# Two mask buffers, and the mask's DMAs issued by ScalarE

## The chip, the cores and the metric

The kernel runs on one core of a Trainium2 chip. The metric is the device time of one execution in microseconds (us). The engines are PE (TensorE: matmuls into PSUM), DVE (VectorE), ACT (ScalarE), POOL (GpSimd) and SP (SyncE, which here only issues DMAs). Each runs its own list of instructions in order. They wait for each other by semaphores, which count up.

## The reference, cut to what matters

A deformable convolution on 8 images of 16 x 16 pixels and 64 channels is followed by an attention and a mixture of experts on the tokens. Only the convolution matters here:

```
xdw    = depthwise_conv3x3(group_norm(x)) + dw_b
om     = xdw @ om_w + om_b            # per pixel, 8 groups, 9 taps: offset x, offset y, mask
value  = group_norm(x) @ vp_w + vp_b  # 8 groups of 8 channels
for each group g, tap k, pixel:
    sample value[g] bilinearly at (pixel + tap k + offset), zero outside the image
    out[g] += sample * mask[g, k]
x = x + out @ op_w
```

## The kernel before, in words

The bilinear weights are written as hats: the weight of image row y is max(0, 1 - |py - y|), and the same for columns. For an image, `a` holds the hats of rows for 128 partitions (8 groups x 16 rows), 9 taps and 256 pixels; `b` holds those of columns. `a` is also multiplied by the mask, so that the sum over rows and columns is the whole of the convolution.

For image n the steps are:

- PE multiplies `om_w` by the convolved image, in two halves (`offsets`, line 272). ACT copies them with a bias to `om_f` (`copy_offsets`, line 488) and rounds them to `om_r` (`high_offsets`, line 502); POOL makes the rest of the rounding (`low_offsets`).
- The mask is part of `om_f`. Three DMAs (`masks`, line 233) bring it to the 128 partitions of `mask`: three taps each, 384 KB, where each of 8 source rows goes to 16 partitions. SP issues them.
- PE spreads the offsets to the partitions in nine steps (`replicate`) through one bank, `ps_m`. ACT copies each out as |.| (`copy_rep`) and makes the hat (`hat`). Five of the nine fill `a`, in pairs of taps.
- POOL multiplies a pair of taps of `a` by `mask` (`masked`, line 762), when the hat is there and the mask's DMA has landed.
- SP copies each pair of `a` to `a_rep` by four DMAs (`fill`, line 241), each from 32 partitions to 128. There are two buffers, by the image's parity. 16 of the 20 DMAs have 256 KB, the last pair's four 128 KB.
- PE samples columns into PSUM (`sample`), DVE multiplies by `a_rep` (`weight`, 18 products an image, line 663), and PE sums over rows into `ps_d` (`reduce`).

The order is written out by hand. While PE, DVE and ACT are at image i, PE puts the spreading of image i + 1 between its batches (`JOBS`, line 195), and ACT and POOL make `a` and `b` of image i + 1. SP's list is: masks of image n, fills of image n, masks of n + 1, and so on. With one `mask`, the masks of image n + 1 may be written only when POOL has done the last multiplication of image n; SP's place behind the last `fill` of image n, which waits for `a_done`, sees to this. ACT writes `om_f` of image n only when the masks of image n - 1 have landed (`mask_in`, line 494) and when POOL has done all multiplications of image n - 1 (`a_done`, line 495).

Tile names: `ps_t`, `ps_m`, `ps_d` are in PSUM, `prod` holds products; `om_copied` counts halves of `om_f`, `a_done` pairs multiplied by the mask, `weighted` products.

Of the kernel before, what the change touches and what calls it, by code (L numbers as in the profile page):

```python
# [27 lines left out]
ALU = mybir.AluOpType  # L28
# [3 lines left out]
P = 128  # L32
IMAGES, H, W, C = 8, 16, 16, 64
PIX = H * W
TT = IMAGES * PIX // P
TPI = PIX // P
GROUPS = 8
GC = C // GROUPS
TAPS = 9
# [4 lines left out]
QUADS = 3  # L44
# [3 lines left out]
MASK_ROWS = [slice(0, 64, 8), slice(1, 64, 8), slice(64, 114, 7)]  # L48
PLACE_ROWS = {0: [r for r in range(64) if r % 8 > 1], 64: [r for r in range(64, 120) if r % 7 != 1 or r > 113]}
BANK = 512  # L50
PAIRS = (TAPS + 1) // 2
# [8 lines left out]
def positive(value):  # L60

    return not isinstance(value, int) or value > 0

def count(eng, value):

    return value if isinstance(value, int) else eng.snap(value)

def spread(ap, dim, n):  # L70

    ap = ap.unsqueeze(dim)
    return ap.broadcast_to([n if k == dim else size for k, size in enumerate(ap.shape)])
# [18 lines left out]
def conv_stage(nc, d, t_tok, pack, pack_in):  # L92

    with ExitStack() as ctx:
        def sb(name, shape, dt=F32, where=ctx):
            return where.enter_context(nc.sbuf_tensor(name, shape, dt))

        def sem(name):
            return ctx.enter_context(nc.semaphore(name))  # L100
# [35 lines left out]
        om_f = sb("om_f", [P, QUADS, PIX])  # L136
# [2 lines left out]
        vt = [sb(f"vt{i}", [P, 2, DUO, H, 4]) for i in range(2)]  # L139
        a = sb("a", [P, TAPS, PIX])  # L140
        b = [sb(f"b{i}", [P, TAPS, PIX]) for i in range(2)]
        mask = sb("mask", [P, TAPS, PIX])
        a_rep = [sb(f"a_rep{i}", [P, DUOS, TAPS, PIX]) for i in range(2)]
        prod = [sb(f"prod{i}", [P, 2, BANK]) for i in range(PROD)]
        d_sb = sb("d_sb", [P, BANK])
# [21 lines left out]
        om_copied = sem("om_copied")  # L167
# [10 lines left out]
        a_done = sem("a_done")  # L178
        b_done = sem("b_done")
        mask_in = [sem(f"mask_in{j}") for j in range(QUADS)]  # L180
# [34 lines left out]
        def pair_taps(k):  # L215

            return slice(2 * k, min(2 * k + 2, TAPS))
# [7 lines left out]
        @block.sync  # L225
        def _(sp):
            sp.dma_start(x_turned[:, :, :, :].rearrange("p s y x -> p (s y x)"), d["x_turned"]).then_inc(x_in, 16)
            sp.dma_start(keep[:, :], d["keep"]).then_inc(keep_in, 16)
            sp.dma_start(start[:, :], d["start"]).then_inc(start_in, 16)
            sp.dma_start(t_tok[:, :, :], xview).then_inc(tokens_in, 16)  # L230
            sp.dma_start(pack[:, :], d["attention"]).then_inc(pack_in, 16)

            def masks(n):

                sp.wait_ge(om_copied, 2 * n + 2)
                for j in range(QUADS):
                    src = om_f[MASK_ROWS[j], :, :].rearrange("g q x -> g (q x)")
                    sp.dma_start(mask[:, QUADS * j:QUADS * (j + 1), :].rearrange("p q x -> p (q x)"),
                                 src.unsqueeze(1).broadcast_to([GROUPS, P // GROUPS, QUADS * PIX])).then_inc(mask_in[j], 16)

            def fill(n, par):

                used = count(sp, WPI * (n - 1))
                if positive(used):
                    sp.wait_ge(weighted, used)
                for k in range(PAIRS):
                    sp.wait_ge(a_done, PAIRS * n + k + 1)
                    for m in range(DUOS):
                        src = a[32 * m:32 * m + 32, pair_taps(k), :]
                        sp.dma_start(a_rep[par][:, m, pair_taps(k), :],  # L250
                                     src.unsqueeze(1).broadcast_to([32, 4, src.shape[1], PIX]))\
                          .then_inc(a_filled[k][m // 2], 16)

            masks(0)
            fill(0, 0)
            masks(1)
            fill(1, 1)
            with sp.Fori(1, IMAGES // 2) as it:
                for par in range(2):
                    masks(2 * it + par)  # L260
                    fill(2 * it + par, par)

        @block.tensor
# [207 lines left out]
        def _(act):  # L471
# [16 lines left out]
            def copy_offsets(half, n):  # L488
                act.wait_ge(om_ps, 2 * n + half + 1)
                if positive(2 * n + half - 1):  # L490
                    act.wait_ge(om_low, 2 * n + half - 1)
                if positive(n) and half == 0:
                    for j in range(QUADS):
                        act.wait_ge(mask_in[j], 16 * n)
                    act.wait_ge(a_done, PAIRS * n)
                bank = ps_m[:, :] if positive(n) else ps_t[0][:, half, :]
                for q in range(2 - half):
                    op = act.activation(om_f[0:ROWS, 2 * half + q, :], bank[0:ROWS, q * PIX:(q + 1) * PIX],  # L498
                                        ACT.Identity, bias=om_bias[0:ROWS, 2 * half + q:2 * half + q + 1])
                op.then_inc(om_copied, 1)  # L500

            def high_offsets(half, n):
                act.wait_ge(om_copied, 2 * n + half + 1)
                if positive(len(REPS) * n):
                    act.wait_ge(rep_ps, len(REPS) * n)
                act.activation(om_r[0:ROWS, 2 * half:2 + half, :], om_f[0:ROWS, 2 * half:2 + half, :],
                               ACT.Copy).then_inc(om_high, 1)
# [67 lines left out]
            def image(i, par, slab, made):  # L575
                n, npar = i + 1, 1 - par
                if made:
                    copy_offsets(0, n)
                    high_offsets(0, n)
                last = None if isinstance(i, int) and i == 0 else i - 1  # L580
                if LAG == 1 and last is not None:
                    copy_d(last)
                if made:
                    copy_offsets(1, n)
                    high_offsets(1, n)
                if LAG == 2 and last is not None:
                    copy_d(last)
                if made:
                    reps(n, npar, slab)
# [9 lines left out]
            high_offsets(0, 0)  # L599
            copy_offsets(1, 0)  # L600
            high_offsets(1, 0)
            first_reps()
            image(0, 0, 1, True)
            image(1, 1, None, True)
# [127 lines left out]
        @block.gpsimd  # L732
        def _(pool):
            pool.memset(minus_half[:, :], -0.5).then_inc(zeroed, 1)
            pool.memset(xpad[:, :, :, :], 0.0).then_inc(zeroed, 1)
            pool.wait_ge(zeroed, 2)
            pool.wait_ge(gn_steps, 5)
            pool.tensor_tensor(grstd[:, :], gvar_eps[:, :], minus_half[:, :], ALU.pow).then_inc(gn_pow, 1)

            def low_offsets(half, n):  # L740

                if half == 0 and positive(n):
                    pool.wait_ge(a_done, PAIRS * n)
                pool.wait_ge(om_high, 2 * n + half + 1)
                q = slice(2 * half, 2 + half)
                pool.tensor_tensor(om_r[64:ROWS, q, :], om_f[64:ROWS, q, :], om_r[64:ROWS, q, :].bitcast(F32),
                                   ALU.subtract).then_inc(om_low, 1)

            def tables(n, par, slab):

                pool.wait_ge(keep_in, 16)
                pool.wait_ge(om_low, 2 * n + 2)
                pool.wait_ge(v_done, slab + 1)
                if positive(WPI * (n - 1)):
                    pool.wait_ge(sampled, WPI * (n - 1))
                for j in range(DUO):
                    op = pool.tensor_tensor(vt[par][:, :, j, :, :].rearrange("p h y c -> p y h c"),
                                            v_sb[:, :, par, j, :].rearrange("p y (h c) -> p y h c", h=2),
                                            spread(spread(spread(rows[:, j], 1, H), 2, 2), 3, 4), ALU.mult)
                op.then_inc(vt_ready, 1)  # L760

            def masked(k, n, par):

                pool.wait_ge(a_hat, PAIRS * n + k + 1)
                for j in range(2 * k // QUADS, min(2 * k + 1, TAPS - 1) // QUADS + 1):
                    pool.wait_ge(mask_in[j], 16 * (n + 1))
                v = a[:, pair_taps(k), :]
                pool.tensor_tensor(v, v, mask[:, pair_taps(k), :], ALU.mult).then_inc(a_done, 1)  # L768

            def image(n, par, slab):  # L770
                low_offsets(0, n)
                low_offsets(1, n)
                tables(n, par, slab)
                for k in range(PAIRS):
                    masked(k, n, par)

            image(0, 0, 0)
            image(1, 1, 0)
            image(2, 0, 1)
            with pool.Fori(1, IMAGES // 2 - 1) as it:  # L780
                image(2 * it + 1, 1, it)
                image(2 * it + 2, 0, it + 1)
            image(IMAGES - 1, 1, SLABS - 1)
# [849 lines left out]
```

## Time and profile before

| | us |
|---|---|
| median of 3 runs (476.04 to 477.93) | 477.06 |
| the profiled execution | 478.97 |
| its span in the trace | 477.1 |
| busy: PE / DVE / ACT / POOL | 406.5 / 331.4 / 237.9 / 136.3 |
| products of DVE, line 674: 128 of them | 152.6, 1.219 each |

The convolution takes the span's first 276 us, the tokens the rest. A busy share is an average over both. What an engine waited for, and when, is read from its rows in order of time, where a bracket tells the idle time ahead of a row and what ended it.

### The profile page before, as it was taken

The page shows a single profiled execution, that of the slowest core. Times are in us where ns is not written, and L with a number is a line of the kernel's source. Part 1 is how long each engine was busy: PE and PEld are TensorE (multiplying, and loading weights), DVE is VectorE, ACT ScalarE, POOL GpSimd, SP SyncE. Part 2 cuts the span into 40 slices and gives each one's busy share as a digit, 9 for nine tenths or more (in the row PEclk, how much of TensorE's full clock was granted, in tenths as well). Part 3 has the DMA queues.
Part 4 walks back from the last instruction along what each step waited for, and adds up shares of the span by engine and source line. Part 5 has one row for each costly group of instructions (what it writes and reads, how often), then busy time and mean ns, then how long its engine had stood idle before and what let it go on. Part 6 is the DMA issues. An engine that isn't in the chain of part 4 may idle for free. (4 is left out here: it accounts for less than half of the span.)

```text
span 477.1 us, 9502 instructions
## 1 busy us (share of the span) xinstructions
PE 406.5 (85%) x3188; PEld 222.6 (47%) x3188; DVE 331.4 (69%) x725; ACT 237.9 (50%) x528; POOL 136.3 (29%) x172
## 2 busy tenths in 40 slices
PE   0739989799999899998969745899999999999995
PEld 0612343332433324332323234776676767777673
DVE  3417978569886498876957845668696967768653
ACT  3543544335544256353530034567767676776752
POOL 2242160421503315133040044223332323223322
PEclk9967999979999599998987955589999999999998
DMA  7178687796976968869789060000000000000000
GB/s 215 31 181 222 154 217 209 159 247 143 231 210 154 237 155 218 217 140 229 170 201 239 14 264 1 0 3 0 2 3 11 2 0 3 12 0 3 12 0 13
DMA packets 31672, 53.94 MB, mean 113 GB/s; under 512 B 7056, under 2 KB 11280, under 8 KB 31376
## 3 DMA queue, kind: packets, MB, share of 16 engines
q1 hardware_dynamic: 31632, 53.43, 43.7%
q8 instruction: 22, 0.36, 0.3%
q14 instruction: 18, 0.15, 0.1%
HBM read 5.71 MB, written 0.52 MB: 13 GB/s over the span
## 5 line engine op out<-in xcount | busy, mean ns | idle before, releaser
L674 DVE TENSOR_TENSOR prod<-ps_t,a_rep 128x1024 f32<-128x1024 f32 x128 | 152.6, 1219 | 56.3 <-DMA a_rep<-a 31.4
L768 POOL TENSOR_TENSOR a<-a,mask 128x512 f32<-128x512 f32 (+1 forms) x40 | 46.5, 1179 | 140.2 <-DMA mask<-om_f 125.6
L373 PE MATMUL ps_t<-b,vt 32*128 32x512 f32 x512 | 80.4, 700 | 6.3 <-DVE prod L674 6.2
L393 PE MATMUL ps_d<-prod,keep 128*32 128x512 f32 x512 | 73.1, 645 | 1.2 <-DVE prod L674 0.9
L1222 POOL TENSOR_TENSOR total<-total,share 128x256 f32<-128x256 f32 x56 | 40.9, 730 | 87.6 <-DVE share L1116 87.3
L1100 DVE TENSOR_TENSOR hidden<-ps_h,gated 128x256 f32<-128x256 f32 x128 | 51.4, 415 | 4.0 <-ACT gated L1315 2.4
L1315 ACT ACTIVATE gated<-ps_h 128x256 f32<-128x256 f32 x128 | 47.8, 387 | 8.2 <-PE ps_h L1435 1.9
L520 ACT ACTIVATE a<-ps_m 128x512 f32<-128x512 f32 x28 | 16.7, 598 | 58.8 <-PE ps_m L314 58.8
L1435 PE MATMUL ps_h<-xf,w_h 128*128 128x256 f32 x128 | 44.1, 344 | 2.0 <-ACT gated L1315 2.0
L1116 DVE TENSOR_TENSOR share<-ps_yf,factor 128x256 f32<-128x256 f32 x56 | 23.7, 423 | 30.9 <-issue 12.8
L1309 ACT ACTIVATE factor<-ps_yf 128x256 f32<-128x256 f32 x64 | 24.6, 385 | 37.9 <-PE ps_yf L1470 37.9
L1470 PE MATMUL ps_yf<-hidden,w 128*64 128x256 f32 x256 | 42.2, 409 | 0.0
L314 PEld LDWEIGHTS ps_m<-om_r,sel 128*128 128x128 f32 x128 | 19.5, 192 | 48.3 <-issue 32.1
L373 PEld LDWEIGHTS ps_t<-b,vt 32*128 32x128 f32 x512 | 21.7, 197 | 34.2 <-DVE prod L674 20.1
L1435 PEld LDWEIGHTS ps_h<-xf,w_h 128*128 128x128 f32 x128 | 25.0, 195 | 27.0 <-issue 21.5
L1435 PE MATMUL ps_h<-xf,w_l 128*128 128x256 f32 x128 | 37.0, 289 | 0.0
L1444 PE MATMUL ps_h<-xf,w_h 128*128 128x256 f32 x128 | 36.6, 287 | 0.0
L1444 PE MATMUL ps_h<-xf,w_l 128*128 128x256 f32 x128 | 36.6, 286 | 0.0
L314 PE MATMUL ps_m<-om_r,sel 128*128 128x256 f32 x128 | 32.6, 337 | 0.0
L283 PE MATMUL ps_m<-conv,start 64*128 64x256 f32 x42 | 14.7, 461 | 19.3 <-ACT om_f L498 16.7
L520 ACT ACTIVATE b<-ps_m 128x512 f32<-128x512 f32 x28 | 16.7, 597 | 28.7 <-PE ps_m L314 28.7
L1466 PE MATMUL ps_yf<-dispatch,select 128*128 128x256 f32 x64 | 23.8, 372 | 5.8 <-DVE t_tok L1122 3.3
(149 smaller groups left out, 641.9 us busy)
## 6 DMA issues: line engine op xcount, KB each, us to landing
a_rep<-a SPq DMA_DIRECT2D x128, 256.0 KB, 4.9
mask<-om_f SPq DMA_DIRECT2D x24, 384.0 KB
a_rep<-a SPq DMA_DIRECT2D x32, 128.0 KB, 3.2
w_f<-in_w SPq DMA_DIRECT2D x2, 1024.0 KB, 5.8
start<-in_start SPq DMA_DIRECT2D x1, 960.0 KB, 7.5
x_turned<-in_x_turned SPq DMA_DIRECT2D x1, 512.0 KB, 3.5
t_tok<-in_x SPq DMA_DIRECT2D x1, 512.0 KB, 8.7
w<-in_w SPq DMA_DIRECT2D x1, 512.0 KB, 7.6
```

The lines of the kernel that those rows point to most:

```text
L314: mm = pe.matmul(bank[:, s * PIX:(s + 1) * PIX], sel[:, tap % 3 + 3 * axis, :], om_r[:, tap // 3, :], start=True, stop=True)
L373: mm = pe.matmul(out, vt[par][r, v % 2, :, :, :].rearrange("p j y c -> p (j y c)"), b[par][r, pair_taps(v // 2), :].rearrange("p t x -> p ...
L393: mm = pe.matmul(ps_d[r, :], fold[:, v % 2, :], p, start=v == 0, stop=False, skip_group_check=True)
L520: act.activation(dst[:, pair_taps(k), :].rearrange("p t x -> p (t x)"), ps_m[:, :], ACT.Abs)\
L674: dve.tensor_tensor(p[:, :, :], t[:, :, :], a_rep[par][:, ms, pair_taps(v // 2), :].rearrange("p m t x -> p m (t x)"), ALU.mult).then_inc( ...
L768: pool.tensor_tensor(v, v, mask[:, pair_taps(k), :], ALU.mult).then_inc(a_done, 1)
L1100: dve.tensor_tensor(hidden[u % 4][:, :], ps_h2[u % 2][:, 0:PIX], gated[u % 4][:, :], ALU.mult)\
L1222: pool.tensor_tensor(sums[:, :], sums[:, :], share[p % 2][:, :], ALU.add).then_inc(added, 1)
L1315: act.activation(gated[u % 4][:, :], ps_h1[u % 2][:, 0:PIX], ACT.Silu).then_inc(silu_done, 1)
L1435: mm = pe.matmul(ps_h1[u % 2][:, 0:PIX], w[:, e, :], tokens, start=first, stop=not first)
L1444: mm = pe.matmul(ps_h2[u % 2][:, 0:PIX], w[:, e, :], tokens, start=first, stop=not first)
L1470: mm = pe.matmul(ps_y[64 * k:64 * k + 64, :], w3[:, u % EXPERTS, :], hidden[u % 4][:, :], start=True, stop=True)
```

## The change

`mask` becomes two buffers, chosen by the image's parity. The function `masks` moves from SP to ACT, where it stands behind the second half's rounding of the same image; for image 0 it stands there too, ahead of the first copies. ACT's wait for `a_done` before it writes `om_f` of image n becomes one for the multiplications of image n - 2, whose mask buffer will be written next. Sizes, sources and the number of DMAs stay.

```diff
-        mask = sb("mask", [P, TAPS, PIX])
+        mask = [sb(f"mask{i}", [P, TAPS, PIX]) for i in range(2)]
...
-            def masks(n):
-
-                sp.wait_ge(om_copied, 2 * n + 2)
-                for j in range(QUADS):
-                    src = om_f[MASK_ROWS[j], :, :].rearrange("g q x -> g (q x)")
-                    sp.dma_start(mask[:, QUADS * j:QUADS * (j + 1), :].rearrange("p q x -> p (q x)"),
-                                 src.unsqueeze(1).broadcast_to([GROUPS, P // GROUPS, QUADS * PIX])).then_inc(mask_in[j], 16)
-
...
-            masks(0)
             fill(0, 0)
-            masks(1)
             fill(1, 1)
             with sp.Fori(1, IMAGES // 2) as it:
                 for par in range(2):
-                    masks(2 * it + par)
                     fill(2 * it + par, par)
...
-                    act.wait_ge(a_done, PAIRS * n)
+                    if positive(PAIRS * (n - 1)):
+                        act.wait_ge(a_done, PAIRS * (n - 1))
...
+            def masks(n, par):
+
+                act.wait_ge(om_copied, 2 * n + 2)
+                for j in range(QUADS):
+                    src = om_f[MASK_ROWS[j], :, :].rearrange("g q x -> g (q x)")
+                    act.dma_start(mask[par][:, QUADS * j:QUADS * (j + 1), :].rearrange("p q x -> p (q x)"),
+                                 src.unsqueeze(1).broadcast_to([GROUPS, P // GROUPS, QUADS * PIX])).then_inc(mask_in[j], 16)
...
                 if made:
                     copy_offsets(1, n)
                     high_offsets(1, n)
+                    masks(n, npar)
...
             high_offsets(1, 0)
+            masks(0, 0)
             first_reps()
...
-                pool.tensor_tensor(v, v, mask[:, pair_taps(k), :], ALU.mult).then_inc(a_done, 1)
+                pool.tensor_tensor(v, v, mask[par][:, pair_taps(k), :], ALU.mult).then_inc(a_done, 1)
```

ACT's list at the start of an image inside the loop, before: both halves of the offsets, then the first copy of `a`.

```order
L498 ACTIVATE om_f<-ps_m,om_bias 120x256 [waits mask_in1,mask_in2,mask_in0,a_done,om_low,om_ps]
L498 ACTIVATE om_f<-ps_m,om_bias 120x256
L506 ACTIVATE om_r<-om_f 120x512 [waits rep_ps,om_copied]
L538 ACTIVATE d_sb<-ps_d 128x512 [waits reduced]
L498 ACTIVATE om_f<-ps_m,om_bias 120x256 [waits om_low,om_ps]
L506 ACTIVATE om_r<-om_f 120x256 [waits rep_ps,om_copied]
L520 ACTIVATE a<-ps_m 128x512 [waits a_filled0_1,a_filled0_0,rep_ps]
L532 ACTIVATE a<-a 128x512 [waits rep_out]
```

The same place now (line numbers are those of the changed kernel):

```order
L488 ACTIVATE om_f<-ps_m,om_bias 120x256 [waits mask_in1,mask_in2,mask_in0,a_done,om_low,om_ps]
L488 ACTIVATE om_f<-ps_m,om_bias 120x256
L504 ACTIVATE om_r<-om_f 120x512 [waits rep_ps,om_copied]
L536 ACTIVATE d_sb<-ps_d 128x512 [waits reduced]
L488 ACTIVATE om_f<-ps_m,om_bias 120x256 [waits om_low,om_ps]
L504 ACTIVATE om_r<-om_f 120x256 [waits rep_ps,om_copied]
L497 DMA mask<-om_f 128x1x768 [waits om_copied]
L497 DMA mask<-om_f 128x1x768 x2
L518 ACTIVATE a<-ps_m 128x512 [waits a_filled0_1,a_filled0_0,rep_ps]
L530 ACTIVATE a<-a 128x512 [waits rep_out]
```

Three DMAs have come between the second rounding and the first copy of `a`; the wait for `a_done` in the first row is now for an image earlier.

SP's list from the last fills of an image to the first of the next, before:

```order
L250 DMA a_rep<-a 128x1x256 [waits a_done]
L250 DMA a_rep<-a 128x1x256 x3
L235 ISA
L238 DMA mask<-om_f 128x1x768 [waits om_copied]
L238 DMA mask<-om_f 128x1x768 x2
L245 REGISTER_ALU
L247 ISA [waits weighted]
L250 DMA a_rep<-a 128x1x512 [waits a_done]
L250 DMA a_rep<-a 128x1x512 x3
```

The same place now:

```order
L242 DMA a_rep<-a 128x1x256 [waits a_done]
L242 DMA a_rep<-a 128x1x256 x3
L237 REGISTER_ALU
L239 ISA [waits weighted]
L242 DMA a_rep<-a 128x1x512 [waits a_done]
L242 DMA a_rep<-a 128x1x512 x3
```

The three DMAs of `mask` and the wait for `om_copied` are gone from SP, so that the fills of one image stand right behind those of the image before.

## Rows read from the trace of the kernel before

**Rows 1.** The page's 40 slices of the span: busy tenths of the DMA engines.

```profile
DMA  7178687796976968869789060000000000000000
```

**Rows 2.** DVE in order of time: start, us, instruction, count, idle ahead.

```profile
33.83 1.23 DVE L674 TENSOR_TENSOR prod<-ps_t,a_rep 128x1024 f32<-128x1024 f32 x1 [9.53 <-DMA a_rep<-a]
...
94.83 1.22 DVE L674 TENSOR_TENSOR prod<-ps_t,a_rep 128x1024 f32<-128x1024 f32 x1 [4.58 <-DMA a_rep<-a]
...
166.28 1.23 DVE L674 TENSOR_TENSOR prod<-ps_t,a_rep 128x1024 f32<-128x1024 f32 x1 [1.67 <-PE ps_t L373]
...
185.46 1.21 DVE L678 TENSOR_TENSOR prod<-ps_t,a_rep 128x1024 f32<-128x1024 f32 x1
186.60 2.34 DVE L674 TENSOR_TENSOR prod<-ps_t,a_rep 128x1024 f32<-128x1024 f32 x2
...
194.73 2.35 DVE L674 TENSOR_TENSOR prod<-ps_t,a_rep 128x1024 f32<-128x1024 f32 x2 [0.72 <-PE ps_t L373]
...
210.42 2.36 DVE L678 TENSOR_TENSOR prod<-ps_t,a_rep 128x1024 f32<-128x1024 f32 x2 [0.21 <-PE ps_t L378]
...
246.42 1.22 DVE L674 TENSOR_TENSOR prod<-ps_t,a_rep 128x1024 f32<-128x1024 f32 x1 [4.34 <-DMA a_rep<-a]
```

**Rows 3.** Waits: who waited for whom, us in total, times, longest.

```profile
POOL a L768 <- DMA mask<-om_f: 125.6, 23, 17.0
...
DVE prod L674 <- DMA a_rep<-a: 31.4, 13, 9.5
...
ACT om_f L498 <- POOL a L768: 20.5, 6, 6.4
```

**Rows 4.** SP's queue in order of time; the second row is from a narrower window.

```profile
80.37 4.01 SPq L238 DMA_DIRECT2D mask<-om_f  x3
...
81.05 3.33 SPq L238 DMA_DIRECT2D mask<-om_f  x2
...
87.71 22.18 SPq L250 DMA_DIRECT2D a_rep<-a  x20
110.04 4.00 SPq L238 DMA_DIRECT2D mask<-om_f  x3
...
276.56 0.82 SPq L967 DMA_DIRECT2D w_f<-in_w  x2
```

**Rows 5.** POOL's multiplications by the mask in one image, in order of time.

```profile
86.41 1.28 POOL L768 TENSOR_TENSOR a<-a,mask 128x512 f32<-128x512 f32 x1 [15.43 <-DMA mask<-om_f]
90.51 2.51 POOL L768 TENSOR_TENSOR a<-a,mask 128x512 f32<-128x512 f32 x2 [2.83 <-DMA mask<-om_f]
93.61 1.95 POOL L768 TENSOR_TENSOR a<-a,mask 128x512 f32<-128x512 f32 x2 [0.59 <-DMA mask<-om_f]
```

**Rows 6.** Windows: length, five engines' busy us, granted clock, DMA share, GB/s.

```profile
83.00:89.00 6.00, 6.00 (x54) 2.31 (x46) 5.65 (x5) 2.63 (x7) 1.28 (x1) 1.00 0.49 101
94.00:109.00 15.00, 12.10 (x66) 4.53 (x70) 9.78 (x11) 5.30 (x10) 4.31 (x6) 0.77 0.90 242
...
109.00:113.00 4.00, 3.89 (x32) 1.22 (x28) 3.93 (x6) 1.98 (x4) 0.00 (x0) 1.00 0.67 177
...
94.00:124.00 30.00, 26.44 (x172) 9.42 (x172) 24.55 (x28) 13.30 (x26) 8.69 (x10) 0.89 0.79 200
```

**Rows 7.** ACT in order of time, around the second rounding in three images.

```profile
19.16 0.42 ACT L506 ACTIVATE om_r<-om_f 120x256 fp32r<-120x256 f32 x1
21.06 0.60 ACT L547 ACTIVATE a<-ps_t 128x512 f32<-128x512 f32 x1 [1.48 <-PE ps_t L314]
...
98.25 0.42 ACT L506 ACTIVATE om_r<-om_f 120x256 fp32r<-120x256 f32 x1
104.80 0.60 ACT L520 ACTIVATE a<-ps_m 128x512 f32<-128x512 f32 x1 [6.14 <-PE ps_m L314]
...
195.21 0.60 ACT L520 ACTIVATE a<-ps_m 128x512 f32<-128x512 f32 x1 [4.73 <-PE ps_m L314]
```

**Rows 8.** Window, PE alone: length, busy us, granted clock, DMA share, GB/s.

```profile
95.00:103.00 8.00, 6.52 (x26) 0.57 0.91 242
```

## The prediction

> **What bounds the kernel now.** I read the slices of the page first. DMA is busy in the deformable convolution, slices 3 to 24 of 40, and near zero behind it [rows 1]; the change touches the convolution alone, so what follows its last product stays as it is.
>
> Next the period: the first product of image 0 starts at 33.83 and that of image 7 at 246.42, so 212.6 us for seven images, **30.4 us an image** [rows 2]. An image in which no product waits for a DMA is image 5: from 186.60 to 210.42 + 2.36 = 212.78, 26.2 us. Images 2 and 4 have the nine steps of the depthwise convolution on DVE as well; from their fifth product to their last it takes 185.46 + 1.21 - 166.28 = 20.4 us where image 5 takes 212.78 - 194.73 = 18.05, so some 28.6 in all. What PE and DVE need is thus (5 x 26.2 + 2 x 28.6) / 7 = 26.9 us, and 3.5 us an image are lost.
>
> Then the waits. POOL's multiplication by the mask waits 125.6 us for the mask's DMA in 23 waits, the products 31.4 us for `a_rep` in 13, ACT's `om_f` 20.5 us for POOL [rows 3]. The circle is seen in SP's queue [rows 4]: three masks from 80.37 to 84.38, nothing until 87.71, then 20 fills until 109.89, and at once the next three masks. POOL can multiply from 86.41, when the first mask is in, though `a` is ready long before (it sits idle for 15.43 us) [rows 5]. So masks and fills take turns, by SP's order alone. That looks like 3.3 us of empty queue per image, which the change takes away.
>
 Three masks of 384 KB are 1.18 MB: at 101 GB/s 11.7 us, of which SP's empty 3.3 us are a part. From 94 to 124, about one period (94.83 to 125.43), the share is 0.79: 23.7 us of all engines, of which masks are 0.49 x 11.7 = 5.7, so fills 18.0. The half that carries the masks has **11.7 + 18.0 = 29.7 us of work in a period of 30.4**. It is the bound, and SP's queue only decides in which order it works. The 0.7 us left over are where fills run out before the masks start: share 0.67 from 109 to 113.
>
> The Trainium skill, "DMA: Bandwidth & Descriptors", section "Why a DMA increments its semaphore by 16 and not by 1", says that the number of engines follows from the slowest dimension on both sides and is at most one that divides both; the masks' source has eight rows there. This would be eight engines, the half that the share shows, and the source is left as it is, so by this rule the half stays the bound; a sum by the empty queue of SP would give 3.3 us an image instead.
>
> **The change part by part.**
>
> *The three masks leave SP.* SP issues 3 DMAs less per image, 4.01 us of its queue [rows 4], and waits no more for `om_copied` between two fills. Its 20 fills of 22.18 us then follow each other as `a_done` comes. Nothing else is behind the masks on SP; what was moved past are the fills of the image before. A fill of image n can now start while image n-1 is computed, bounded by `weighted` of image n-2.
>
> *ACT issues them.* Behind the second rounding, at 98.25 + 0.42 = 98.67, ACT does nothing until 104.80, when the first copy of the next image has its bank [rows 7]. In image 5 this gap is 4.73 us. SP paid 4.01 us for three masks: the first took 4.01 - 3.33 = 0.68, the other two 3.33, since what is not yet sent holds them up [rows 4]. Below I bound ACT's cost by SP's plain issues of weights, 0.82 us for two [rows 4], 1.2 us for three; above by the whole landing, 80.37 to 93.61, 13.2 us. I take the row of the same DMA, 4.0 us, which lies within 4.7. What is queued behind it is the copy of the first `a` bank, and PE's next spreading needs that bank one batch later, about 2.5 us (two products, 2.36, and a gap). So up to 4.7 + 2.5 = 7.2 us are free; an issue of 13.2 us would cost 6.0 us an image. Cost taken: 0.
>
> *At the start* ACT issues at 19.58 and does so for 4 us, where it was idle for 1.48 before the first bank [rows 7]: so its copies come 2.5 us later. DVE's first product waits 9.53 us for `a_rep` [rows 2], whose chain goes by the mask. Cost 0, and 0.4 us if the masks start behind the rounding.
>
> *The wait for `a_done` of the image before becomes one for two images before.* ACT's `om_f` waited 20.5 us for it. It comes early enough now; but ahead of it the half of the engines is full, so this is a wait that moves to DMA and no gain of its own. The second buffer costs no time, only space.
>
> *What DMA gains.* Masks are issued about 4 us into an image, while fills are still under way, so that the half with the masks has both at once. First, it no longer runs dry between fills and masks: 0.7 us an image. Second, a transfer may cost less, or more, beside another kind. No row has both kinds on the same engines. The nearest: the third mask, beside fills on the other half, comes 3.1 us behind the second (93.61 - 90.51), while the second, alone for the most part, took 4.1 us behind the first (90.51 - 86.41) [rows 5]. So some 1.0 us can be had when something else is going on. Above, the gain is limited by 26.9 us an image, 3.5 us; below, two streams on one engine might cost as much as that mask gained for each of three masks, -3 us. I take +1.0, the nearest row.
>
> *Sum.* (0.7 + 1.0) x 7 images = 12 us. The profiled execution took 478.97 us (span 477.1), so 467; it was 1.9 us above the median of 477.06, which gives **465 us**. PE's clock: at 94.83, behind the wait for DMA, PE runs at a granted 0.57 from 95 to 103, mostly the lower level of 1.2 GHz [rows 8]. While the DMA half is the bound, what the clock costs lies beside a wait, and I count nothing for it.
>
> **The rivals.**
>
> *A: forecast.* The half with the masks stays the bound, 28.7 us an image: 458 to 474 us.
>
> *B: only the order was the bound.* With both queues filled, masks and fills overlap so well that PE and DVE set the pace, 26.9 us an image: 7 x 3.5 = 24.5 us off 477, 453. For it: 3.3 us of empty SP queue, half of the engines idle in the masks' time, restarts at half clock. Against it: 29.7 of 30.4 us on the same half, unless packets of both kinds get cheaper by 10%.
>
> *C: nothing to gain.* The half is full and remains so, and what is won in its gap is lost again: 477, within 0.5% or 2.4 us, which is about what a measurement can tell from no change. If only the gap is won, 7 x 0.7 = 5 us, it is 472 and counts as A. The same page of the Trainium skill, under "Issuing engines are not separate DMA queues", says that DMAs from several engines run on the same 16 engines and that a second issuer saves only sequencer time; by it the gain is what SP loses in issuing, and with the half full that is next to nothing. The trace neither shows nor denies it, having one issuer.
>
> *D: slower.* Masks from ACT compete with the fills that DVE is waiting for. Before, a fill ran behind the masks with its half to itself; now each fill shares it. Place: `a_rep`'s landing in every image. Price: the -3 us above leave 29.7 + 3 = 32.7 us an image, 2.3 above 30.4, so 16 us, 493; it decides as soon as sharing costs over 0.7 us an image, 2% of the half's work. For it: fills alone already give only 242 GB/s with the engines at 0.90, so that they hinder each other. Against it: the third mask's 3.1 us. A long stand of ACT would have to exceed 7.2 + 3.5 us to lose anything, so it is no likely way here.
>
> **How the numbers follow.** A 0.52, B 0.14, C 0.16, D 0.18. Faster is A and B, 0.66; same C, 0.16; slower D, 0.18. The range goes from the middle of B to the near end of D: 453 to 481, with 0.07 below and 0.12 above; A's own range is 458 to 474.
>
> **What would show it.** In the windows: no more stretches with a share of 0.49; a share of 0.83 or more over an image; if A is right, products still wait for `a_rep`, in the middle of images rather than at their start, 10 to 20 us in all. SP's queue has no pause of 3 us. POOL waits for the mask 2 to 6 us instead of 15. ACT's gap behind the second rounding is filled by three DMAs and its first copy starts at most 2 us later in the image. If B is right the waits of the products for `a_rep` vanish behind image 0 and the granted clock stays near 1.00. I am wrong if the share over an image falls while waits for `a_rep` grow (D), or if ACT's issue takes over 7 us and PE waits for its banks.

## The result and the profile after

The median is 479.0 us (477.1 to 482.17) against 476.71 for the kernel before on the same chip (474.94 to 481.06): ratio 1.0049, interval 1.0026 to 1.0072. That is half a per cent slower, 2.3 us, where 12 us less were forecast. The profiled execution of the changed kernel took 477.93 us, span 476.1, and so lies below its median by 1.1 us; the one of before lies above its own. The traces can therefore tell where the 12 us stayed, but not well where the 2.3 us come from.

The waits that were forecast to go have gone. First the list of waits of the kernel after; columns as in [rows 3].

```profile
POOL a L768 <- DMA mask<-om_f: 69.2, 16, 7.7
...
POOL a L768 <- ACT a L530: 31.7, 12, 4.5
...
ACT a L518 <- DMA a_rep<-a: 28.2, 7, 5.6
...
ACT a L518 <- issue: 24.1, 4, 6.1
...
DVE prod L674 <- DMA a_rep<-a: 15.4, 6, 9.4
...
PE ps_m L303 <- ACT a L518: 14.1, 7, 3.4
```

POOL waits 69.2 us for the mask instead of 125.6, the products 15.4 us for `a_rep` instead of 31.4 [rows 3]. In their place ACT's copies into the one `a` wait 28.2 us for fills of the image before, which they did not once in the kernel before, and PE waits 14.1 us for ACT.

SP's queue in order of time, which in [rows 4] went by turns:

```profile
26.32 235.88 SPq L242 DMA_DIRECT2D a_rep<-a  x160
```

All 160 fills follow each other. And ACT in image 2, the place of [rows 7]; the bracket is the idle time and what ended it:

```profile
101.14 0.42 ACT L504 ACTIVATE om_r<-om_f 120x256 fp32r<-120x256 f32 x1
101.14 6.24 ACTq L497 DMA_DIRECT2D mask<-om_f  x3
107.63 0.60 ACT L518 ACTIVATE a<-ps_m 128x512 f32<-128x512 f32 x1 [6.08 <-issue]
...
119.76 0.60 ACT L518 ACTIVATE a<-ps_m 128x512 f32<-128x512 f32 x1 [5.38 <-DMA a_rep<-a]
```

The three issues fill ACT's gap: its first copy starts 107.63 - 101.14 = 6.5 us behind the rounding, before 104.80 - 98.25 = 6.5. What ended the idle time is new, though. Before, ACT waited for PE; now, in this image and three others, its own issues hold it up, and in three of these four PE stands idle for the copy:

```profile
108.28 0.50 PE L303 MATMUL ps_m<-om_r,sel 128*128 128x256 f32 x2 [1.30 <-ACT a L518]
...
172.86 0.50 PE L303 MATMUL ps_m<-om_r,sel 128*128 128x256 f32 x2 [1.12 <-ACT a L518]
...
229.58 0.50 PE L303 MATMUL ps_m<-om_r,sel 128*128 128x256 f32 x2 [1.28 <-ACT a L518]
```

That is 3.7 of the 14.1 us that PE waits for ACT; the rest comes from copies like the last row above, which wait for fills.

Yet nothing has become faster. DVE's products of the kernel after; the first products of images 0, 1 and 7 answer to those of [rows 2]:

```profile
33.64 1.23 DVE L674 TENSOR_TENSOR prod<-ps_t,a_rep 128x1024 f32<-128x1024 f32 x1 [9.36 <-DMA a_rep<-a]
...
44.25 1.23 DVE L674 TENSOR_TENSOR prod<-ps_t,a_rep 128x1024 f32<-128x1024 f32 x1 [2.54 <-issue]
...
52.44 1.22 DVE L674 TENSOR_TENSOR prod<-ps_t,a_rep 128x1024 f32<-128x1024 f32 x1 [3.91 <-issue]
...
66.62 2.36 DVE L674 TENSOR_TENSOR prod<-ps_t,a_rep 128x1024 f32<-128x1024 f32 x2
...
249.10 4.81 DVE L674 TENSOR_TENSOR prod<-ps_t,a_rep 128x1024 f32<-128x1024 f32 x4 [0.61 <-PE ps_t L362]
```

The lengths of the images, from first product to first product (the last to the end of its last product), in us:

| image | 0 | 1 | 2 | 3 | 4 | 5 | 6 | 7 | mean of 1 to 6 |
|---|---|---|---|---|---|---|---|---|---|
| before | 30.2 | 30.8 | 30.6 | 29.9 | 31.3 | 29.1 | 30.7 | 26.5 | 30.39 |
| after | 33.0 | 30.9 | 31.8 | 32.9 | 29.4 | 27.3 | 30.1 | 23.0 | 30.41 |

The period is what it was. Image 0 has become 2.7 us longer, with two new idle times of DVE, 2.54 and 3.91 us, for which the profile names no releaser. Image 7 is 3.6 us shorter: its `a_rep` is there, DVE doesn't restart behind a wait, and from 246.40 to 255.00 PE's granted clock is 1.00 where it was 0.50.

Now the DMA engines over images 1 to 6, the columns of [rows 6]. After:

```profile
66.60:249.10 182.50, 164.78 (x1540) 64.23 (x1544) 139.41 (x137) 81.05 (x160) 51.76 (x54) 0.96 0.82 194
```

The same six images of the kernel before:

```profile
64.10:246.40 182.30, 166.29 (x1540) 63.84 (x1532) 138.39 (x135) 82.13 (x159) 51.66 (x56) 0.94 0.78 195
```

The rate is equal, 194 and 195 GB/s, since the same bytes take the same time; but the engines are busy for 0.82 instead of 0.78. Per image that is 0.82 x 30.41 - 0.78 x 30.39 = 1.2 us more for the same transfers, or 0.9 to 1.5 with the rounding of the shares. The page's slices and its queues (packets, MB, share of 16 engines) say so too:

```profile
DMA  7178898797877878869889070000000000000000
...
q1 hardware_dynamic: 28368, 44.00, 37.3%
q10 hardware_dynamic: 3264, 9.44, 8.2%
```

(37.3 + 8.2)% of 476.1 is 216.6 us. Before, one queue carried all:

```profile
q1 hardware_dynamic: 31632, 53.43, 43.7%
```

43.7% of 477.1 is 208.5 us, 8 us less for eight images' transfers. The engines look busier, as forecast, and move no more.

### The profile page after: what moved, and what is told of

The parts are those of the page before. It is cut to its first block and busy times, and to the rows that moved or that the text cites. A ratio compares the mean times of both kernels' runs of the same rounds, so it can differ in the third digit from the quotient of the medians.

```text
span 476.1 us, 9495 instructions
## 1 busy us (share of the span) xinstructions
PE 401.9 (84%) x3188; PEld 220.6 (46%) x3188; DVE 332.0 (70%) x725; ACT 237.4 (50%) x528; POOL 136.7 (29%) x172
## 3 DMA queue, kind: packets, MB, share of 16 engines
q1 hardware_dynamic: 28368, 44.00, 37.3%
## 5 line engine op out<-in xcount | busy, mean ns | idle before, releaser
L362 PE MATMUL ps_t<-b,vt 32*128 32x512 f32 x512 | 77.7, 677 | 6.0 <-DVE prod L674 5.9
L382 PE MATMUL ps_d<-prod,keep 128*32 128x512 f32 x512 | 72.0, 636 | 4.7 <-DVE prod L674 4.7
L768 POOL TENSOR_TENSOR a<-a,mask 128x512 f32<-128x512 f32 (+1 forms) x40 | 46.9, 1181 | 101.3 <-DMA mask<-om_f 69.2
L518 ACT ACTIVATE a<-ps_m 128x512 f32<-128x512 f32 x28 | 16.7, 597 | 76.9 <-DMA a_rep<-a 28.2
L1116 DVE TENSOR_TENSOR share<-ps_yf,factor 128x256 f32<-128x256 f32 x56 | 23.7, 423 | 30.8 <-issue 12.8
L303 PE MATMUL ps_m<-om_r,sel 128*128 128x256 f32 x128 | 33.0, 340 | 14.1 <-ACT a L518 14.1
L746 POOL TENSOR_TENSOR om_r<-om_f,om_r 56x512 fp32r<-56x512 f32 (+1 forms) x16 | 15.8, 1000 | 59.2 <-ACT om_r L504 59.0
```

What stands on the lines that cost most here:

```text
L303: mm = pe.matmul(bank[:, s * PIX:(s + 1) * PIX], sel[:, tap % 3 + 3 * axis, :], om_r[:, tap // 3, :], start=True, stop=True)
L362: mm = pe.matmul(out, vt[par][r, v % 2, :, :, :].rearrange("p j y c -> p (j y c)"), b[par][r, pair_taps(v // 2), :].rearrange("p t x -> p ...
L382: mm = pe.matmul(ps_d[r, :], fold[:, v % 2, :], p, start=v == 0, stop=False, skip_group_check=True)
L768: pool.tensor_tensor(v, v, mask[par][:, pair_taps(k), :], ALU.mult).then_inc(a_done, 1)
```

## The experiments

All but the fifth were timed beside the kernel before, on one chip for each group; a ratio compares the two sets of runs and need not be the quotient of the medians shown. The theory at the start, H: masks with eight source rows keep one half of the engines busy, and that half bounds the convolution whoever issues. Rivals: something about the order, the second buffer or ACT's issue sets the period.

**1. Two buffers alone, masks still from SP.** From the kernel before:

```diff
-        mask = sb("mask", [P, TAPS, PIX])
+        mask = [sb(f"mask{i}", [P, TAPS, PIX]) for i in range(2)]
...
-                    act.wait_ge(a_done, PAIRS * n)
+                    if positive(PAIRS * (n - 1)):
+                        act.wait_ge(a_done, PAIRS * (n - 1))
```

> The kernel before with two mask buffers and ACT's wait for the multiplications of two images before, but the mask DMAs still issued by SP between the fills. Theory H (half of the DMA engines, which carries masks and fills, is full, whatever the order): within 0.5% of before, 474.5 to 479. Theory I (the change loses by ACT standing 4 to 6.4 us in its mask issues): the same, 474.5 to 479, with the changed kernel's loss absent. Theory O (order alone was the bound and the earlier om_f helps): 465 to 472.

Measured: 477.68 against 477.21, ratio 0.9997 (0.9957 to 1.0037), 30.38 us an image. The buffer and the looser wait do nothing that can be measured, so what the change does lies in the issue by ACT.

**2 and 3. Masks read from 16 source rows, issued by ACT and by SP.** The edit is the same in the changed kernel (2) and in the kernel before (3), here that of 2:

```diff
-                    src = om_f[MASK_ROWS[j], :, :].rearrange("g q x -> g (q x)")
+                    src = om_f[j:64:4, :, :].rearrange("g q x -> g (q x)")
...
-                                 src.unsqueeze(1).broadcast_to([GROUPS, P // GROUPS, QUADS * PIX])).then_inc(mask_in[j], 16)
+                                 src.unsqueeze(1).broadcast_to([16, P // 16, QUADS * PIX])).then_inc(mask_in[j], 16)
```

> The changed kernel, with each mask DMA read from 16 rows of om_f instead of 8, same bytes, same number of DMAs, same queue. The rows are other rows than the mask's, so the masks hold other numbers; all else is computed. Theory H: mask DMAs spread over all 16 engines, so the full half has 18.0 + 5.9 = 24 us of work an image instead of 30, PE and DVE set the pace at about 26.9 us, time 451 to 458, products hardly wait for a_rep behind image 0. Theory I: ACT's stand gets shorter with shorter queues, at most 1.5 us an image back: 468 to 479. If neither engines nor stand matter (fills and the single a buffer bound it): 476 to 482.

> The kernel before (one mask, SP issues) with the mask DMAs read from 16 rows instead of 8; the masks hold other numbers. Theory H: the masks take half the time on all engines, 5.9 us, so the half that was full has 24 us, and SP's serial order (masks, landing, multiplication, fills of 22 us) sets the pace at 27 to 28.5 us an image: 455 to 466. Theory O (SP's order is the bound, engines are not): the wait between masks and fills shrinks by at most 1 us an image, 468 to 477.

Measured: from ACT 454.59, ratio 0.9535 (0.9478 to 0.9592), 27.39 us an image; from SP 450.58, ratio 0.9429 (0.9378 to 0.948), 26.93 us an image. Bytes and number of DMAs are the same, only the rows read differ. A window of the run from SP, in the columns of [rows 6]:

```profile
60.00:220.00 160.00, 156.01 (x1527) 60.89 (x1527) 137.11 (x135) 80.09 (x156) 51.69 (x54) 1.00 0.91 221
```

All engines can carry the masks now: a share of 0.91, 221 GB/s instead of 195, and PE is busy for 156 of 160 us at the upper level of its clock. In SP's queue the pause behind the masks is still there:

```profile
72.85 2.65 SPq L238 DMA_DIRECT2D mask<-om_f  x3
78.25 21.45 SPq L250 DMA_DIRECT2D a_rep<-a  x20
```

From 75.50 to 78.25 SP issues nothing, and the kernel loses nothing by it. H holds: when the masks use all engines, the period falls to the 26.9 us that PE and DVE were reckoned to need, with the old order and one buffer. The run from SP is even below the 455 to 466 that was expected under H. And once half of the engines is no longer the bound, masks from ACT are worse than from SP, by 4.0 us.

**4. Small masks from ACT.** In the changed kernel the masks of image 2 and later carry 64 of 768 elements:

```diff
+                    if not (isinstance(n, int) and n < 2):
+                        src = om_f[MASK_ROWS[j], 0, 0:64]
+                        act.dma_start(mask[par][:, QUADS * j, 0:64],
+                                      src.unsqueeze(1).broadcast_to([GROUPS, P // GROUPS, 64])).then_inc(mask_in[j], 16)
+                        continue
```

> The changed kernel, where from image 2 on each mask DMA brings 64 elements per partition instead of 768 (1/12 of the bytes, same number of DMAs and rows); the masks of later images are therefore mostly those of images 0 and 1. Theory H: the full half has 18 + about 2 us an image, so 451 to 458, as with 16 rows. Theory F (fills, SP's issue of 20 of them and the single a are the bound): 474 to 482.

Measured: 462.87, ratio 0.9669 (0.9611 to 0.9727), 27.56 us an image. Images 1 to 6, in the columns of [rows 6]:

```profile
70.00:235.00 165.00, 158.56 (x1540) 62.42 (x1540) 139.94 (x135) 81.00 (x158) 51.56 (x54) 1.00 0.74 181
```

It is the masks' work on the engines that costs, not their number. With the engines at 0.74 instead of 0.91, the period isn't shorter than with whole masks from 16 rows (27.39 from ACT), so that there too the pace was set by something other than the DMA engines; PE is busy for 158.56 of 165 us. The time lies above the 451 to 458 that was expected under H. Image 0 took 36.1 us here, some 6 more than in the kernel before: its masks and those of image 1 are whole and come from ACT.

**5. The DMAs alone.** A kernel that holds nothing but these DMAs, three images of each kind in turn: fills alone, masks of 8 rows alone, both from SP's queue by turns, both at once from SP and ACT, masks of 16 rows alone, then these with fills at once. One execution. The heart of it:

```diff
+            for r in range(ROUNDS_M):
+                eight(sp, r, masked[1])
+                fill(sp, r, fills[1])
+            sp.wait_ge(masked[1], NM)
+            sp.wait_ge(fills[1], NF)
+            for r in range(ROUNDS_M):
+                fill(sp, r, fills[2])
...
+            act.wait_ge(masked[1], NM)
+            act.wait_ge(fills[1], NF)
+            for r in range(ROUNDS_M):
+                eight(act, r, masked[2])
```

> Only DMAs of this kernel's shapes, nothing computed (the output is zeros): in turn, each after the one before has landed: 60 fills on SP; 9 masks of 8 rows on SP; three times 3 masks and 20 fills on SP in one queue; 60 fills on SP with 9 masks on ACT at the same time; 9 masks of 16 rows on SP; 60 fills on SP with 9 masks of 16 rows on ACT. By the sums of the prediction: fills 54 to 57 us, masks 35 us at a DMA share of 0.5, one queue 89 to 92 us. Both at once is the disputed size: if a transfer gets cheaper beside another kind (the prediction's +1.0 us an image) 83 to 87 us; if the half's work merely adds up 89 to 92; if it gets dearer on shared engines 92 to 98. Masks of 16 rows alone 17 to 20 us at a share of 0.9 or more; with fills 70 to 77 us.

SP's queue (first the whole run, then the rows of a narrower window from 95), and ACT's:

```profile
3.45 64.28 SPq L1638 DMA_DIRECT2D a_rep<-a  x60
69.75 33.76 SPq L1644 DMA_DIRECT2D mask<-om_f  x12
...
282.69 14.49 SPq L1650 DMA_DIRECT2D mask<-om_f  x9
302.26 81.32 SPq L1638 DMA_DIRECT2D a_rep<-a  x60
385.58 0.39 SPq L1686 DMA_DIRECT2D out<-a  x1
```

```profile
99.61 3.90 SPq L1644 DMA_DIRECT2D mask<-om_f  x3
103.57 25.54 SPq L1638 DMA_DIRECT2D a_rep<-a  x20
129.15 3.98 SPq L1644 DMA_DIRECT2D mask<-om_f  x3
133.17 26.13 SPq L1638 DMA_DIRECT2D a_rep<-a  x20
159.35 3.96 SPq L1644 DMA_DIRECT2D mask<-om_f  x3
```

```profile
192.41 21.96 ACTq L1644 DMA_DIRECT2D mask<-om_f  x9
```

Windows of its stretches: length, POOL's busy time, clock, DMA share, GB/s. In order: fills alone, 8 rows alone, one queue, two queues, 16 rows alone, 16 rows with fills. Those of one queue and of two hold all three images; the others leave out start and end.

```profile
4.00:66.00 62.00, 0.00 (x0) 1.00 0.88 217
72.00:95.00 23.00, 0.00 (x0) 1.00 0.49 131
99.61:192.41 92.80, 0.00 (x0) 1.00 0.78 191
192.41:282.69 90.28, 0.00 (x0) 1.00 0.82 196
285.00:300.00 15.00, 0.00 (x0) 1.00 0.97 200
304.00:383.00 79.00, 0.00 (x0) 1.00 0.91 218
```

By image: fills alone (69.75 - 3.45) / 3 = 22.1 us; masks of 8 rows (99.61 - 69.75) / 3 = 9.95 us at a share of 0.49; masks of 16 rows (302.26 - 282.69) / 3 = 6.5 us at 0.97. By turns in one queue, from one set of masks to the next, 129.15 - 99.61 = 29.5 and 159.35 - 129.15 = 30.2 us. That is nearly the kernel's 30.4, with no compute engine at work. With both queues, 90.3 us for three images (192.41 to 282.69), where one queue took 92.8 (99.61 to 192.41): 0.8 us an image are won. It isn't quite the kernel's order, since ACT issues all nine masks at once here. The engines are busy for 0.82 x 90.28 - 0.78 x 92.80 = 1.6 us more, some 0.5 an image, for the same bytes. So here too they cost more on two queues, but less than the better order gives; in the kernel nothing is left of the gain. Fills and masks of 16 rows at once took (385.58 - 302.26) / 3 = 27.8 us an image up to the store of the output at 385.58, start and end included: at 16 rows the engines have little room left either.

**6. Rows doubled, masks from 16 rows, results kept.** For each of three groups of taps a small DMA first copies the 8 mask rows to 16 of a new tile `mini`; the mask's DMA then reads those. In 6a SP issues the small ones ahead of the last four fills, in 6b ACT does, behind its second rounding; the masks stay on SP and in one buffer. The core of 6b, from the kernel before:

```diff
-                    src = om_f[MASK_ROWS[j], :, :].rearrange("g q x -> g (q x)")
+                    sp.wait_ge(mini_in[j], 16 * (n + 1))
+                    src = mini[0:64:4, j, :]
...
-                                 src.unsqueeze(1).broadcast_to([GROUPS, P // GROUPS, QUADS * PIX])).then_inc(mask_in[j], 16)
+                                 src.unsqueeze(1).broadcast_to([16, P // 16, QUADS * PIX])).then_inc(mask_in[j], 16)
...
+            def twice(n):
...
+                    act.dma_start(mini[0:64:4, j, :],
+                                 src.unsqueeze(1).broadcast_to([GROUPS, 2, QUADS * PIX])).then_inc(mini_in[j], 16)
```

> The kernel before (one mask, SP), with each mask's 8 rows first copied by a small DMA to 16 rows of a new tile, every fourth partition, issued on SP ahead of the last pair's fills of the image before; the three mask DMAs then read 16 rows. All is computed. Theory H (the eight-row source fills half of the engines): 450 to 458, near the 450.6 of the run with 16 rows on SP. If the small DMAs or their landing cost more than about 1 us an image: 458 to 466.

> The same, but the small DMAs are issued by ACT behind its second rounding. Theory H: 450 to 458 too; ACT's three issues, some 2 us, lie within its gap of 4.7 us. If every DMA issued on ACT there costs what the 16-row run on ACT lost against the one on SP (4 us): 454 to 462.

Measured: 6a 465.2, ratio 0.9766 (0.972 to 0.9813), 28.58 us an image; 6b 461.0 (456.53 to 462.1), ratio 0.9665 (0.9602 to 0.9728), 27.9 us. Both lie above the 450 to 458 expected under H, and within what was expected if the small DMAs cost something (458 to 466, and 454 to 462). 6b is faster than both kernels. The small DMAs on ACT's queue are the kind of issue that the change put there, but they replace work of the bounding half instead of reordering it:

```profile
62.85 3.50 ACTq L514 DMA_DIRECT2D mini<-om_f  x3
90.86 3.79 ACTq L514 DMA_DIRECT2D mini<-om_f  x3
```

**7. The masks of image 1 from SP.** If image 0's 2.7 us come from the masks of image 1 overtaking fills that DVE awaits, SP should issue those masks behind the fills of image 0 and leave the rest to ACT. In the changed kernel:

```diff
+            masks(1, 1)
...
-                    masks(n, npar)
+                    if not (isinstance(n, int) and n == 1):
+                        masks(n, npar)
```

> The changed kernel, except that the masks of image 1 are issued by SP behind the fills of image 0, as before; all other images' masks by ACT. In the trace of the changed kernel image 0 takes 33.0 us instead of 30.25 and the six images behind it the same 30.4. If the early masks of image 1, ahead of fills that products wait for, are the loss: image 0 at 30 to 31 us and a time 2 to 3 us below the changed kernel's, 474 to 478. If ACT's standing in its issues is the loss: no change against the changed kernel, 478 to 480.

Measured: 480.36, ratio 1.0093 (1.0046 to 1.0139), above both expectations and no gain on the changed kernel's 1.0049. Image 0 is back at 30.7 us, but image 1 takes 34.9, the others 30.1 to 31.0 and the last 23.0. DVE in image 1 of this run:

```profile
74.30 3.49 DVE L684 TENSOR_TENSOR prod<-ps_t,a_rep 128x1024 f32<-128x1024 f32 x3 [0.68 <-DMA a_rep<-a]
83.56 2.36 DVE L684 TENSOR_TENSOR prod<-ps_t,a_rep 128x1024 f32<-128x1024 f32 x2 [5.78 <-DMA a_rep<-a]
```

So the place was right (here the profile names `a_rep`), and the hope was wrong: by this trace the loss moves to the first image in which ACT's masks, 4.77 us of issue from 65.88 on, run beside fills that are awaited.

## Why the prediction was wrong, by its own steps

- *The bound*: right. One half of the engines with 29.7 us of work in 30.4. Alone, the same transfers take 29.5 to 30.2 us an image. The two terms were off, and it is luck that their errors nearly cancelled: fills 18.0 forecast, 0.86 x 22.1 = 19.0 measured alone, with the share from 3.45 to 69.75; masks 11.7, 9.95 alone. (Slice 24 of the page, which the prediction gives to the convolution, is the load of `w_f` at 276.56 [rows 4]; nothing hangs on it.)
- *The floor of PE and DVE*, 26.9 us: right. Experiment 3 has 26.93, with PE busy for 156 of 160 us.
- *"It no longer runs dry: 0.7 us an image"*: not seen. SP's queue has no pause and the period is the same to 0.02 us. In the DMAs alone two queues save 0.8 us, both gains together, where 1.7 were forecast.
- *"I take +1.0, the nearest row"*: this step failed most, its sign too. The third mask came sooner, but that the fills beside it were the reason was never shown: masks alone differ as much from one window to the next (last section). What shares the same engines costs more: 1.2 us an image of engine time in the kernel, some 0.5 in the DMAs alone. In the kernel nothing is left of what the better order gives, so it is rival C, "what is won in its gap is lost again", with a little of D. Why the kernel has none of the 0.8 us that the DMAs alone win isn't shown. The waits behind ACT's issues and for the single `a` (below) are a candidate.
- *The rule weighed under C*: the Trainium skill, "DMA: Bandwidth & Descriptors", section "Issuing engines are not separate DMA queues", says that a second issuer saves only sequencer time. The DMAs alone agree to 0.8 us of 30.9. C, the rival beside which it stands, had a chance of 0.16. The same page's rule on the number of engines ("Why a DMA increments its semaphore by 16 and not by 1") agrees with 0.49 for 8 rows and 0.97 for 16.
- *ACT's issue*: 4.0 us taken, 4.06 to 6.41 in the trace. The 7.2 us "free" were too many: behind issues of 6.24, 6.06 and 6.41 us PE waited 1.30, 1.12 and 1.28 for the first copy, so that about 5 us were free there. And the forecast had no term for the single `a`: with the fills further behind, ACT's copies wait 28.2 us for it and PE some 10 of its 14.1. What these waits cost beside the full half isn't shown, and a second `a` was not tried. Experiments 2 and 3, without the full half, differ by 4.0 us, of which 0.46 x 6 = 2.8 lie in images 1 to 6.
- *Image 0*: not counted. The prediction named "masks from ACT compete with the fills that DVE is waiting for" under D, in every image; it happened in one, 2.7 us.
- *What would show it*: share 0.82 (0.83 asked), no pause of SP, POOL's waits 69.2 / 16 = 4.3 us, ACT's gap filled. The waits for `a_rep` are 15.4 us (10 to 20 asked), but 9.4 of them stand before the first product of image 0 and not in the middle of images. Most came as written, and the time didn't. The list tested whether the order changes, not whether the bound shrinks; share times period at equal bytes would have been the sign.

What stays open, beside the 0.8 us: why the median is 2.3 us higher (1.2 to 3.4). The profiled execution gets image 0's 2.7 us back in image 7, and one trace can't tell whether the others do.

## What to carry to other kernels

When two streams take turns on a resource that is full, the pauses in a queue aren't losses: add up the resource's work per period first, and expect little of an order that leaves this sum alone. Here the sum fell by a change of shape, 16 source rows instead of 8 for the same bytes. Read busy share with bytes moved beside it, since here a share that rose at a constant rate (0.78 to 0.82, 195 and 194 GB/s) was more time for the same bytes and no progress.

## What the runs showed of the hardware that I had not expected

- The masks from 16 rows use all engines (0.97 against 0.49) but go at 200 GB/s against 131, 1.5 times as fast and not twice.
- Three issues of masks hold ACT for 4.06 to 6.41 us, SP for 4.0 [rows 4]; three small DMAs of 48 KB written each still hold ACT for 2.48 to 3.90 us.
- The rate of a short window isn't the rate of a stretch. In the DMAs alone, windows of 6 us among the eight-row masks, in the columns above, differ by half at an even share:

```profile
74.00:80.00 6.00, 0.00 (x0) 1.00 0.49 110
80.00:86.00 6.00, 0.00 (x0) 1.00 0.50 134
86.00:92.00 6.00, 0.00 (x0) 1.00 0.50 160
```

The 11.7 us forecast for masks rested on one such window of 6 us, 101 GB/s [rows 6]; over 23 us it is 131.
